# New instruction orders for a woven two-layer transformer kernel, one product moved to GpSimd, two helpers split

## The reference

```python
x = x + tanh(g_xattn[0]) * L0_xattn(layernorm(x), ctx)   # 16 heads of 8, causal mask, softmax
x = x + tanh(g_ffn[0])  * L0_ffn(layernorm(x))           # silu(gate) * up, down; inner width 512
x = x + tanh(g_xattn[1]) * L1_xattn(layernorm(x), ctx)   # each head sees 8 own context tokens
x = x + tanh(g_ffn[1])  * L1_ffn(layernorm(x))           # 16 experts of width 64, top 2, and a shared one of 256
```

## Time and profile before

| | us |
|---|---|
| median of 3 runs | 181.97 (181.89 to 184.7) |
| profiled execution | 181.77 |
| its span, first to last instruction | 179.9 |
| mean granted TensorE clock | 0.978 of full speed |

### The profile page before, as it was taken

One profiled execution on the slowest core, in us unless ns is written; L12 is line 12 of the kernel. 1 busy time (PEld: TensorE's weight loads), 2 busy tenths in 40 slices (PEclk: granted clock), 3 DMA queues, 4 the chain that ended last, 5 costly groups with the idle time before them and its releaser, 6 DMA issues.

```text
span 179.9 us, 3906 instructions
## 1 busy us (share of the span) xinstructions
PE 161.3 (90%) x1443; PEld 98.3 (55%) x1456; DVE 127.6 (71%) x347; ACT 94.7 (53%) x180; POOL 76.5 (43%) x131
## 2 busy tenths in 40 slices
PE   7819999999999989999979584999999999999993
PEld 5513455675454445545647463646575784657572
DVE  0695757976888868896887977675897775746263
ACT  0405677968698685877957457751742134121210
POOL 3683065674679874976997914022002000000000
PEclk9975999999999999999999999999999999999998
DMA  5986000000000000000000000000000000100001
GB/s 166 400 268 292 0 4 0 5 4 4 4 0 4 0 0 4 0 4 2 5 0 0 0 4 0 0 0 5 0 0 0 0 0 4 58 0 0 0 0 58
DMA packets 1889, 5.82 MB, mean 32 GB/s; under 512 B 208, under 2 KB 592, under 8 KB 1744
## 3 DMA queue, kind: packets, MB, share of 16 engines
q1 hardware_dynamic: 1152, 4.01, 6.0%
q10 hardware_dynamic: 720, 1.57, 2.4%
HBM read 5.06 MB, written 0.52 MB: 31 GB/s over the span
## 4 chain that ended last, share of the span: by engine, by line
PE 70%; DVE 11%; ACT 7%; POOL 5%; issue 4%; DMA 2%; another core or an unknown queue 1%; DVEq 0%; POOLq 0%; ACTq 0%
PE banks L1538 10%; PE banks L1512 8%; PE banks L1515 8%; PE banks L1346 6%; PE banks L1355 5%; PE banks L1334 5%; PE banks L1390 4%; PE banks L1393 3%; DVE xn L830 3%; DMA x_all<-in_x 2%; POOL rstd L264 2%; PE banks L1374 2%; PE banks L1528 2%; ACT pT L534 2%; PE banks L1266 2%
## 5 line engine op out<-in xcount | busy, mean ns | idle before, releaser
L901 DVE TENSOR_REDUCE banks<-banks 128x8 f32<-128x1024 f32 x16 | 19.7, 1231 | 10.5 <-PE banks L1346 10.2
L631 ACT ACTIVATE full<-banks 128x512 f32<-128x512 f32 x20 | 11.8, 596 | 28.9 <-PE banks L1512 28.9
L289 POOL TENSOR_SCALAR_AFFINE_SELECT pT<-pT 128x512 f32<-128x512 f32 x32 | 19.9, 635 | 11.4 <-ACT pT L534 11.3
L1538 PEld LDWEIGHTS banks<-ews,rest 128*128 128x128 f32 x160 | 20.0, 192 | 5.1 <-issue 3.6
L1060 DVE TENSOR_TENSOR xnT<-full,banks 128x512 f32<-128x512 f32 x20 | 13.6, 682 | 11.4 <-PE banks L1515 7.8
L1538 PE MATMUL banks<-ews,rest 128*128 128x128 f32 x160 | 20.7, 277 | 0.1
L1512 PE MATMUL banks<-nT,ews 128*128 128x512 f32 x40 | 20.8, 602 | 0.0
L1515 PE MATMUL banks<-nT,ews 128*128 128x512 f32 x40 | 20.4, 592 | 0.0
L534 ACT ACTIVATE pT<-banks 128x512 f32<-128x512 f32 x32 | 17.8, 595 | 4.3 <-PE banks L1374 4.1
L1355 PE MATMUL banks<-qm,kT 32*128 32x512 f32 x64 | 17.9, 640 | 0.0
L1068 DVE TENSOR_TENSOR rest<-xnT,banks 128x512 f32<-128x512 f32 x20 | 13.5, 685 | 4.9 <-PE banks L1538 3.9
(11 more groups left out here) (172 smaller groups left out, 327.2 us busy)
## 6 DMA issues: line engine op xcount, KB each, us to landing
ews<-in_ew SPq DMA_DIRECT2D x1, 1928.5 KB, 7.6
fws<-in_fw SPq DMA_DIRECT2D x1, 768.0 KB, 8.2
cT<-in_ctxT ACTq DMA_DIRECT2D x2, 256.0 KB, 5.4
x_all<-in_x SPq DMA_DIRECT2D x2, 256.0 KB, 4.6
lws<-in_lw ACTq DMA_DIRECT2D x1, 449.0 KB, 8.3
sels<-in_sel ACTq DMA_DIRECT2D x1, 320.0 KB, 8.6
a<-in_aw ACTq DMA_DIRECT2D x1, 256.0 KB, 4.9
out_x<-x_all SPq DMA_DIRECT2D x1, 256.0 KB, 2.0
```

The source lines that it names most:

```text
L289: nc.gpsimd.affine_select(out=probs, in_=probs, compare_op=ALU.is_ge, fill=0.0, base=0, pattern=[[0, HG], [1, S]], channel_multiplier=-1). ...
L901: V.tensor_reduce(bank[2 * p][:, 0:2 * HG], banks[p][:, :].rearrange("p (h k) -> p h k", h=2 * HG), AX.X, ALU.max).then_inc(sm["a_mx"], 1)
L1538: last = mm(bank[t][:, b * D:(b + 1) * D], e_h[:, u, b * S:(b + 1) * S], expert(c)[2], start=(c == 0 and (b == 0 or s == 1 and b == 2)), s ...
```

## The change

Four functions change. The last step of `hidden_steps`, the product of the hidden scale with the scale of `down`, becomes `hidden_dequant` on GpSimd; the statistics behind `ffn_residual` become `ffn_stats`; the product in `heads_out` becomes `heads_scaled`, an instruction that waits as before. So each can stand elsewhere in its list. Then all five lists except SyncE's are ordered anew. No other instruction is added; 15 of the 76 fillers go.

```diff
-        STEPS2 = 4
+        STEPS2 = 3
...
+            def hidden_dequant(m):
+                pool.wait_ge(sm["f_hstep"], STEPS2 * m + 2)
+                pool.wait_ge(sm["w_deq"], 1)
+                nc.gpsimd.tensor_scalar(f_ah[:, m, 3:4], f_ah[:, m, 1:2], fdown[:, 0:1], None,
+                                        ALU.mult).then_inc(sm["f_hd"], 1)
...
                 V.reciprocal(rl[:, :], bank[6 + n % 2][:, S:2 * S]).then_inc(sm["a_rl"], 1)
+
+            def heads_scaled(n):
+
                 dve.wait_ge(sm["a_rl"], n + 1)
...
                 V.reciprocal(f_ah[:, m, 2:3], f_ah[:, m, 1:2]).then_inc(sm["f_hstep"], 1)
-                dve.wait_ge(sm["w_deq"], 1)
-                V.tensor_scalar(f_ah[:, m, 3:4], f_ah[:, m, 1:2], fdown[:, 0:1], None,
-                                ALU.mult).then_inc(sm["f_hstep"], 1)
...
-                dve.wait_ge(sm["f_hstep"], STEPS2 * (m + 1))
+                dve.wait_ge(sm["f_hd"], m + 1)
...
+            def ffn_stats(m):
+
                 dve.wait_ge(sm["f_res"], m + 1)
                 V.bn_stats(tok(stats, m, 6), tok(x_all, m)).then_inc(sm[f"ln_stats{m // HALF}"], 1)
```

GpSimd's list at the start (removed and added lines):

```diff
-            nc.gpsimd.memset(ones_sq[:, :], 1.0).then_inc(sm['const_ok'], 1)
-            nc.gpsimd.memset(ob[:, :, :], 0.0).then_inc(sm['ob_zero'], 1)
-            nc.gpsimd.memset(mhalf[:, :], -0.5).then_inc(sm['const_ok'], 1)
             nc.gpsimd.memset(identb[:, :], 0.0).then_inc(sm['ident_ok'], 1)
-            nc.gpsimd.memset(top2[:, :, :], 3e+38).then_inc(sm['const_ok'], 1)
             nc.gpsimd.memset(maskb[:, :], 0.0).then_inc(sm['ident_ok'], 1)
             ones_and_masks()
-            rstd_of(0, 0)
+            nc.gpsimd.memset(ones_sq[:, :], 1.0).then_inc(sm['const_ok'], 1)
+            nc.gpsimd.memset(mhalf[:, :], -0.5).then_inc(sm['const_ok'], 1)
+            nc.gpsimd.memset(top2[:, :, :], 3e+38).then_inc(sm['const_ok'], 1)
+            nc.gpsimd.memset(vz[:, :, :, :, :], 0.0).then_inc(sm['vz_zero'], 1)
+            nc.gpsimd.memset(ob[:, :, :], 0.0).then_inc(sm['ob_zero'], 1)
             nc.gpsimd.memset(mxs[:, :, :, :], 0.0).then_inc(sm['const_ok'], 1)
             nc.gpsimd.memset(magic[:, 0:1], MAGIC).then_inc(sm['const_ok'], 1)
-            nc.gpsimd.memset(vz[:, :, :, :, :], 0.0).then_inc(sm['vz_zero'], 1)
-            nc.gpsimd.memset(wT[:, :], 0.0).then_inc(sm['wT_zero'], 1)
+            nc.gpsimd.memset(magic[:, 1:2], -MAGIC).then_inc(sm['const_ok'], 1)
+            nc.gpsimd.memset(chosen[:, :, NE:NR], 1.0).then_inc(sm['const_ok'], 1)
+            rstd_of(0, 0)
+            rstd_of(0, 1)
+            ones_of_heads()
             folding_rows()
-            nc.gpsimd.memset(magic[:, 1:2], -MAGIC).then_inc(sm['const_ok'], 1)
-            ones_of_heads()
-            rstd_of(0, 1)
             spread_values(0)
```

ScalarE, at the start and in the bridge from attention to experts:

```diff
+            nc.scalar.activation(tg[:, :], a[:, A_GX:A_GX + 4], ACT.Tanh).then_inc(sm['gates_ok'], 1)
             k_copy(0)
-            nc.scalar.activation(tg[:, :], a[:, A_GX:A_GX + 4], ACT.Tanh).then_inc(sm['gates_ok'], 1)
             xT_copy(0)
-            weights_abs(0)
             q_copy(0)
             first_queries(2)
+            weights_abs(0)
+            weights_abs(1)
             first_queries(3)
-            weights_abs(1)
             weights_abs(2)
             max_copy(0, 0)
             v_copy(0)
+            k_copy(1)
             exp(0, 0)
             exp(0, 1)
-            k_copy(1)
...
+            kq_copy(0)
             hidden_scale(4)
-            gate_tanh(5)
-            tanh_plus_one(5)
+            xT3_copy(0)
             hT_copy(4)
+            hidden_scale(5)
             x_scaled(6)
-            xT3_copy(0)
             xqT_copy(6)
-            kq_copy(0)
-            hidden_scale(5)
+            exp3(0)
             gate_tanh(6)
-            exp3(0)
             up_copy(6)
             tanh_plus_one(6)
+            vo_copy(0)
             hT_copy(5)
             pT3_copy(0)
             x_scaled(7)
-            vo_copy(0)
+            nc.scalar.activation(table[:, 0:1], tg[:, 0:1], ACT.Silu)
+            hidden_scale(6)
             xqT_copy(7)
```

```diff
             transposed_scores(7, 0)
+            transposed_scores(7, 1)
+            subtract_max(7, 0)
             heads(6, 1)
-            h_transposes(3)
-            subtract_max(7, 0)
             max_rows(7, 1)
-            down(3)
-            transposed_scores(7, 1)
             xq_transpose(5)
             subtract_max(7, 1)
+            keys_times_queries(0)
+            gate_up(5)
             y_proj(6)
-            gate_up(5)
             heads(7, 0)
             heads(7, 1)
+            scores3_bias(0)
+            x3_transposes(0)
             h_transposes(4)
-            keys_times_queries(0)
+            scores3(0)
+            y_proj(7)
             down(4)
-            y_proj(7)
-            x3_transposes(0)
+            keep_busy(2, 3)
             xq_transpose(6)
-            scores3_bias(0)
-            keep_busy(2, 4)
-            scores3(0)
             gate_up(6)
             values_times_outputs(0)
-            keep_busy(2, 9)
+            keys_times_queries(1)
             h_transposes(5)
-            keep_busy(2, 2)
             p3_transposes(0)
             down(5)
-            keep_busy(2, 8)
+            keep_busy(2, 2)
             y3_proj(0)
             xq_transpose(7)
-            keys_times_queries(1)
+            values_times_outputs(1)
+            keep_busy(2, 4)
             gate_up(7)
-            values_times_outputs(1)
-            keep_busy(2, 6)
+            keep_busy(2, 5)
             h_transposes(6)
+            keep_busy(2, 3)
             x4_transposes(0)
             down(6)
-            keep_busy(2, 5)
+            keep_busy(2, 2)
             logits(0)
```

More of the change, by code:

```diff
@@ L393, in _ @@
             causal(5, 0)
+            causal(5, 1)
+            hidden_dequant(1)
             x_dequant(3)
             gated_up(2)
-            nc.gpsimd.memset(chosen[:, :, NE:NR], 1.0).then_inc(sm['const_ok'], 1)
-            causal(5, 1)
+            own_tokens(0, 1)
             causal(5, 2)
             causal(5, 3)
-            own_tokens(0, 0)
+            hidden_dequant(2)
             x_prepare(4)
             gated_up(3)
+            own_tokens(1, 0)
+            x_dequant(4)
             causal(6, 0)
-            x_dequant(4)
             causal(6, 1)
+            x_prepare(5)
             causal(6, 2)
+            hidden_dequant(3)
+            gated_up(4)
             causal(6, 3)
-            x_prepare(5)
             x_dequant(5)
-            gated_up(4)
             causal(7, 0)
+            rstd_of(1, 0)
             causal(7, 1)
@@ L1102, in _ @@
             top(3, 0)
+            split_max(3, 0)
             residual(1)
-            split_max(3, 0)
             layer_stats(1)
+            q_masked(1, 3)
             top(3, 1)
-            q_masked(1, 3)
             split_max(3, 1)
+            heads_out(2)
             x_steps(1)
-            heads_out(2)
+            heads_scaled(2)
+            top(4, 0)
+            residual(2)
+            split_max(4, 0)
+            layer_stats(2)
             hidden(0)
-            residual(2)
@@ L1113, in _ @@
             hidden_steps(0)
-            top(4, 0)
-            layer_stats(2)
-            split_max(4, 0)
+            x_steps(2)
+            top(4, 1)
             heads_out(3)
-            weights_clipped(2)
-            top(4, 1)
-            x_steps(2)
             split_max(4, 1)
             hidden(1)
+            heads_scaled(3)
+            hidden_steps(1)
+            top(5, 0)
+            split_max(5, 0)
+            residual(3)
             ffn_residual(0)
-            top(5, 0)
@@ L1125, in _ @@
-            residual(3)
-            split_max(5, 0)
             layer_stats(3)
-            hidden_steps(1)
             top(5, 1)
+            ffn_stats(0)
+            split_max(5, 1)
+            heads_out(4)
             x_steps(3)
-            heads_out(4)
-            split_max(5, 1)
-            ffn_residual(1)
+            heads_scaled(4)
+            top(6, 0)
             residual(4)
             hidden(2)
-            top(6, 0)
+            ffn_residual(1)
+            ffn_stats(1)
@@ L1137, in _ @@
+            split_max(6, 0)
             hidden_steps(2)
-            split_max(6, 0)
             layer_stats(4)
+            top(6, 1)
+            split_max(6, 1)
             heads_out(5)
-            top(6, 1)
             x_steps(4)
-            split_max(6, 1)
+            heads_scaled(5)
             ffn_residual(2)
+            hidden(3)
             residual(5)
-            hidden(3)
+            hidden_steps(3)
+            layer_stats(5)
             top(7, 0)
-            layer_stats(5)
+            top(7, 1)
@@ L1149, in _ @@
             split_max(7, 0)
-            hidden_steps(3)
-            top(7, 1)
+            ffn_stats(2)
+            split_max(7, 1)
+            ffn_residual(3)
+            ffn_stats(3)
             x_steps(5)
-            split_max(7, 1)
```

(17 more changed lines are left out.)

304 lines of the change are left out of this document (154 added, 150 removed).

## The result

| | before | after |
|---|---|---|
| median, us | 182.01 (4 runs) | 176.0 (4 runs, 175.32 to 176.67) |
| profiled execution, its span | 181.77, 179.9 | 176.45, 174.6 |
| granted TensorE clock, mean | 0.978 | 0.971 |

The ratio is 0.967 with a 95% interval of 0.962 to 0.973; ratios here leave out executions over 1.5% above the fastest of the same kernel. Forecast were 173.9, and 171 to 179 as the range: right in the sign, 2.1 us too low. Two of the four executions, at a mean clock of 0.980, took 175.32 and 175.54 us, the two at 0.971 took 176.45 and 176.67.

The account below looks back on a forecast made before the run. TensorE, busy for 90% of the 179.9 us span, was taken as the bound. From 181.77, −5.8 − 1.1 + 0.9 − 2.1 = −8.1 gave 173.7, plus 0.2 for the median: 173.9 us; range 171.0 to 179.0.

Parts of the forecast that it names:

- rival (a): Whole kernel: only the start pays, attention stretch and bridge give back what they gain; 176.2 us, chance 0.19.
- The start, −5.8: Up to the first scores: early memsets free the normalizations, so transposes and scores come sooner; −5.8 us, bounds −7 and −3.5.
- `bn_stats` beside `vz`: Start: the early `vz` memset was taken not to hold the four `bn_stats` it lies beside; cost nothing.
- the 0.9 of the other case: Start: if `vz` did hold the `bn_stats` to 5.7, the start's gain would shrink by 0.9 us.
- Blocks and `keys_times_queries`, −1.1 and +0.9: Attention stretch, TensorE: one score block fewer saves 1.1 us; `keys_times_queries(0)` ahead of the last `heads` adds 0.9.
- The scale on GpSimd, 0: Hidden-scale product moved from VectorE to GpSimd: on no path seen, so 0; bounds −0.5 and +0.8 us.
- The bridge, −2.1: Between attention stretch and last stage: earlier softmax −2.1, values' copy −0.5, memset +0.5; sum −2.1 us, bounds −3.5 and +0.5.
- the values' copy: Bridge: `vo_copy(0)` now ahead of `pT3_copy(0)`, so `y3_proj` no longer waits for it; −0.5 us.
- `wT`'s memset: End of the bridge: behind `gated_up(7)`, it may keep VectorE's normalization out for 0.95 us; half taken, +0.5.
- one of 1.95 was not, and mine are no longer: Bridge: a 1.95 us TensorE gap was not followed by 1.2 GHz and new gaps are no longer, so the clock holds.
- rival b: Bridge: the clock falls for want of fillers, with 2.8 us of loss; 176.7 us, chance 0.05.
- The last stage, 0 (bounds −0.3 and +1.5): Router and experts: same TensorE instructions with 0.4 us idle, again 63.2 us; 0, bounds −0.3 and +1.5.

Follow-up runs that it names:

- e2: The changed kernel with 20 more fillers directly ahead of `x4_transposes(0)`, `wT`'s memset left in place: 172.85 us, ratio 0.953 to the kernel before.
- e6: The kernel before with only the new start of GpSimd's list, plus 20 fillers ahead of `x4_transposes(0)`: 176.9 us, ratio 0.971.
- e3: The kernel before with only GpSimd's list up to the second `rstd_of` as changed, `wT`'s memset behind `folding_rows()`: median 179.53 us.
- e4: The changed kernel with two more neighbours of opposite strips among the score blocks on TensorE: 175.42 us, ratio 0.965 to the kernel before.
- e10: Two more score-block neighbours, on the changed kernel with `wT`'s memset early, `gated_up(7)` held for the normalization and 8 more fillers: 171.04 us, against 171.02 without them.
- e5: The kernel of e2 with the hidden-scale product back on VectorE in `hidden_steps`, no `hidden_dequant`: 172.78 us, ratio 0.952, beside 172.85 for e2.
- e1: The changed kernel with `wT`'s memset moved from behind `gated_up(7)` to behind `folding_rows()` in the start: 174.5 us, ratio 0.961 to the kernel before.
- e13: The changed kernel with `wT`'s memset early, 8 more fillers, `gated_up(7)` and also `gated_up(5)` held for their normalizations: 170.38 us, ratio 0.937 to the kernel before.
- e12: The kernel of e2 with `layer1_normalize(1, n3, 0)` again behind `heads_out(7)` and `heads_scaled(7)`: 174.01 us, ratio 0.956 to the kernel before.
- e9: The kernel of e2 with one more memset, 832 bf16 columns, between `gated_up(7)` and `wT`'s memset: 173.1 us, one execution.

## Why the prediction was right in part

The median lies inside the range, but above the 172.3 to 175.5 that the forecast called its own, and right on the price of rival (a), 176.2. The agreement with (a) is luck: (a) has stretch and bridge give their gain back, while with the clock held (e2) they keep it. Still, as measured the change is worth no more than its start alone in an execution whose clock held (175.96, e6).

- **The start, −5.8: right in mechanism and size.** Normalizations were forecast to take 1.1 us from 7.8 (1.12 from 7.48), transposes at 8.9 (8.65), scores at 12.2 (11.91). The table load even came ahead of its wait, at 3.2. The last `heads` end 6.2 earlier. e3 and e6 show the start alone to be worth 5.7 us up to the bridge and 6.0 in all.
- **`bn_stats` beside `vz`: nothing, as taken.** Four took 0.87 us beside it, 0.88 before; the 0.9 of the other case did not arise.
- **Blocks and `keys_times_queries`, −1.1 and +0.9: the sum was right by accident.** From the first scores to the last `heads` it took 71.45 us and takes 71.65. But e4 and e10 show that saving two more blocks is worth nothing, and their idle time goes to waits for VectorE's maxima; whether the one block that the change itself saved was worth anything is not shown. I took TensorE's share of 96% for a bound; its 3 us of idle said otherwise only when it was tried. By the same token the +0.9 was no sound term.
- **The scale on GpSimd, 0: right** (e5).
- **The bridge, −2.1: near in the sum, off in the parts.** From the last `heads` to `x4_transposes(0)` it took 21.26 us and takes 18.76: −2.5. The softmax starts 4.75 us behind the last `heads` instead of 6.47: −1.7, where −2.1 was forecast. From there to `p3_transposes(0)` it is 4.5 instead of 5.6: −1.1, nearly all of it the softmax product (1.75, now 0.69), which the forecast did not have. To `y3_proj(0)` it is 1.4 instead of 2.2: −0.8, where −0.5 was forecast for the values' copy. From there to the transposes it is 8.1 instead of 7.0: +1.0, where +0.5 was forecast for `wT`'s memset; the memset cost 0.66 (e1), the rest is not assigned.
- **The step that failed: "one of 1.95 was not, and mine are no longer", the clock in the bridge.** The sum has no term for it. The text took gaps of 1.95 us as harmless from one profile, and put the fall of the clock (rival b) at 0.05 and 176.7 us. It is what happened: 176.0 measured, 3.2 us of loss (e2) against 2.8, which was borrowed from the slow start, so that its nearness is luck. The argument was wrong twice: the gap became 2.50, through the very memset that the text named, and gaps of 1.8 to 1.96 had the clock fall in e1, e3 and e6. One profile of before was too little to go by: the kernel before was executed 33 more times beside the experiments, and in 14 of them its mean clock was 0.954 to 0.963 and its time 184.65 to 187.54 us, where the other 19 had 0.972 to 0.990 and 181.11 to 182.53. Where the clock fell in those 14 no trace shows, but the 184.7 us in the table of before was a first sign. With the clock held (e2) the change gives 172.85, 1.1 below the forecast.
- **The last stage, 0 (bounds −0.3 and +1.5): wrong through the same cause.** It took 2.3 us longer in the profiled execution, since it begins at the low level; another 1.3 were lost between `x4_transposes(0)` and `hidden_proj(0)`.

What stays open: why the same gaps let the clock fall in one execution and not in another. No run here shows what decides it.

## What to carry to other kernels

Clear buffers on GpSimd while the first loads are on their way, not beside VectorE's `tensor_scalar` on the critical path; and where a GpSimd instruction has slack, holding it until that `tensor_scalar` is done can be worth more than its early start (e13 against e2: 2.5 us for two waits and a moved memset together). When a change opens or shifts gaps on TensorE, read the granted clock behind each, in more than one execution, before believing a saving: one gap of 2.5 us took back a third of this one. An engine at 96% is not shown to be the bound until a piece of its work has been taken away. And read every instruction on the path that lies beside GpSimd, not only the one that you set out to mend: here the softmax product gave 1.06 us that no term had.

## What the runs showed of the hardware that was not expected

- TensorE came back from gaps of 1.81 (e1), 1.94 (e3), 1.96 (e6) and 2.50 us (the change) in the bridge at a granted clock of 0.50 (1.2 GHz) or fell to it within 0.2 us, and stayed at 1.00 through gaps of 1.95 and 1.94 in the profile of before. In e12 the clock fell 2 us after a gap of 1.37 had ended. In e6 and e3 the first and the second of two like gaps changed roles.
- GpSimd beside a `tensor_scalar` of VectorE can hold it through two instructions back to back (2150 ns, and 4500 before) or let it in between (1259 ns at most in e9). A `tensor_tensor` of VectorE took 1.75 us where GpSimd's started 0.06 us ahead of it, and 0.69 where it started 0.30 us ahead of GpSimd's.
- One loaded table served Silu and Tanh, Identity and Copy: with the dummy Silu at 94.5 no further load stood ahead of `gate_tanh(7)`.
